# First stage of a ternary feed-forward kernel: indices and identities by the vector engine, maxima over partitions by the tensor engine, c of block 0 scaled by a bound, x loaded first

## The reference, cut to what matters

```python
def ternarize(W, threshold):
    absW = jnp.abs(W)
    delta = threshold * jnp.max(absW)
    mask = absW > delta
    n = jnp.maximum(jnp.sum(mask), 1)
    alpha = jnp.sum(jnp.where(mask, absW, 0.0)) / n
    return alpha * jnp.sign(W) * mask
c = jnp.einsum('bct,bcd->bdt', x, weights[conditions])   # weights gathered per batch
h = jnp.einsum('bsd,hd->bsh', c, ternarize(W1, 0.05)) + b1
h = jax.nn.gelu(h, approximate=False)
y = jnp.einsum('bsd,hd->bsh', h, ternarize(W2, 0.05)) + b2
scale = jnp.max(jnp.abs(y)) / 7 + 1e-8
out = x + jnp.clip(jnp.round(y / scale), -7, 7) * scale
```

## Time and profile before

| | us |
|---|---|
| three runs | 1043.31, 1045.27, 1045.33 (median 1045.27) |
| the profiled execution | 1043.61, its span 1041.8 |
| PE busy | 937.6 (90%) |
| DVE busy | 648.8 (62%) |
| ACT busy | 553.8 (53%) |
| POOL busy | 157.8 (15%) |

### The profile page before, as it was taken

The page is one execution under the profiler, slowest core; times in us unless marked ns, Lnnn a source line. Parts: engine busy times, 40 slices in busy tenths (PEclk is TensorE's granted clock), DMA queues, the critical chain, the costliest instruction groups (busy, mean ns, idle before and its releaser), DMA issues.

```text
span 1041.8 us, 15013 instructions
## 1 busy us (share of the span) xinstructions
PE 937.6 (90%) x5265; PEld 448.1 (43%) x5265; DVE 648.8 (62%) x1007; ACT 553.8 (53%) x710; POOL 157.8 (15%) x213
## 2 busy tenths in 40 slices
PE   0499999999999999999999999999999999999600
PEld 0355444444444444444444444444444444444200
DVE  3599766666666656666665666566666656633492
ACT  3489372727456473828274564638282645535290
POOL 4032303030110203030302102030303021000000
PEclk9899999999999999999999999999999999999855
DMA  6610120301121211203011112121030121105999
GB/s 219 201 44 4 30 63 11 70 21 40 45 45 41 50 40 43 48 10 78 13 40 45 45 40 50 40 50 41 10 81 10 40 47 44 40 0 181 307 386 376
DMA packets 40592, 77.89 MB, mean 75 GB/s; under 512 B 3952, under 2 KB 4352, under 8 KB 40064
## 3 DMA queue, kind: packets, MB, share of 16 engines
q1 hardware_dynamic: 36304, 73.47, 24.3%
q0 software_dynamic: 4096, 3.94, 1.4%
q10 hardware_dynamic: 176, 0.27, 0.1%
HBM read 60.89 MB, written 16.78 MB: 75 GB/s over the span
## 4 chain that ended last, share of the span: by engine, by line
PE 77%; issue 10%; ACT 5%; DVE 3%; POOL 2%; DMA 1%; DVEq 0%; ACTq 0%; SPq 0%; POOLq 0%
PE ps L444 38%; PE ps L456 35%; PE ps L432 3%; ACT y L692 2%; PE ps L474 1%; ACT y L664 1%; POOL ws L356 1%; DVE st L709 1%; DMA yx<-in_x 1%; DVE y L822 0%; DVE y L960 0%; ACT ps L692 0%; DVE wts L819 0%; DMA condb<-in_itok_B 0%; DVE st L768 0%
## 5 line engine op out<-in xcount | busy, mean ns | idle before, releaser
L444 PE MATMUL ps<-yc,wts 128*128 128x512 f16 x2048 | 447.3, 379 | 0.3 <-ACT g L596 0.3
L456 PE MATMUL ps<-wts 128*128 128x512 f16 x1920 | 419.3, 379 | 0.7 <-ACT wts L620 0.7
L444 PEld LDWEIGHTS ps<-yc,wts 128*128 128x128 f16 x2048 | 199.4, 98 | 238.7 <-ACT g L596 0.8
L456 PEld LDWEIGHTS ps<-wts 128*128 128x128 f16 x1920 | 185.8, 98 | 220.4 <-ACT wts L620 0.9
L742 DVE SCALAR_TENSOR_TENSOR wts<-g,st,wts 128x512 f16<-128x512 f32 x256 | 186.4, 749 | 143.0 <-ACT wts L601 141.1
L596 ACT ACTIVATE g<-ps,b1t,st 128x512 f32<-128x512 f32 x256 | 197.8, 773 | 116.7 <-PE ps L444 109.3
L601 ACT ACTIVATE wts<-g,st 128x512 f16<-128x512 f32 x256 | 181.0, 713 | 0.0
L583 ACT ACTIVATE xs<-yx,st 128x2048 f16<-128x2048 f32 x28 | 56.1, 2002 | 145.0 <-DVE st L777 145.0
L378 POOL PARTITION_ALL_REDUCE st<-st x46 | 21.5, 467 | 669.1 <-DVE st L711 413.6
L356 POOL DMA_INDIRECT wg<-in_L_cond_weights,ids x112 | 106.5, 951 | 41.3 <-issue 29.3
L747 DVE SCALAR_TENSOR_TENSOR y<-ps,st,b2b 128x512 f32 (+1 forms) x56 | 41.9, 748 | 78.0 <-PE ps L456 78.0
(11 more groups left out here) (118 smaller groups left out, 377.2 us busy)
## 6 DMA issues: line engine op xcount, KB each, us to landing
yx<-in_x SPq DMA_DIRECT2D x56, 512.0 KB, 6.1
out<-wts SPq DMA_DIRECT2D x12, 512.0 KB, 10.2
y<-in_x SPq DMA_DIRECT2D x5, 1024.0 KB, 10.0
wts<-in_x SPq DMA_DIRECT2D x10, 512.0 KB, 6.0
y<-in_L_ffn_W SPq DMA_DIRECT2D x8, 512.0 KB, 9.0
wts<-in_x SPq DMA_DIRECT2D x4, 1024.0 KB, 5.6
y<-in_L_ffn_W SPq DMA_DIRECT2D x4, 1024.0 KB, 8.0
out<-y SPq DMA_DIRECT2D x4, 1024.0 KB, 12.5
```

What stands on the lines that cost most here:

```text
L444: last = nc.tensor.matmul(psH[:, j % HB, :], T1T[:, k, j * P:(j + 1) * P], csp[:, a, k, :], start=(k == 0 and a == 0), stop=(k == KT - 1 a ...
L456: last = nc.tensor.matmul(psY[:, r % 2, :], hsp[:, a, j, r * P:(r + 1) * P], T2T[:, j, :], start=(j == 0 and a == 0), stop=(j == HT - 1 an ...
```

## The change

Everything lies ahead of the loop over blocks, or in the step of block 0.

- x of block 0 is loaded first, in four transfers of 256 KB (two on SP, two on ScalarE's queue after the list of conditions), then W1. W2 follows without a wait. b2's transfer goes behind ScalarE's absolutes.
- VectorE builds indices and identities, by scans, a 32 x 32 transpose and comparisons. GpSimd has no iota, no identity and no reduction of W1's maxima or of c of block 0 any more; it keeps the reduction of b1's.
- The gathers of blocks 0 and 1 are four instructions of 128 rows each instead of eight of 64. No diagonal is cleared. `condition_direct` multiplies 64 rows by 64 columns, sixteen matmuls a half, the two sides of the partitions in two banks.
- The maximum of a column over partitions: VectorE widens it to 128 columns (`wide`), TensorE transposes it (`all_partitions`), VectorE reduces it.
- c of block 0 isn't measured: its scale comes from 128 times the product of the powers of two of max|x| and max|w|. Both parts of it are made from PSUM directly.
- W1's masks come in eight chunks of two tiles (`masks1`). Three turns, not six, stand ahead of `first(0, 0)`, and the counts stand behind first 0, 1 and 2.
- W2's count is made by 32 matmuls (`count2`), ahead of second(0, 0), and ScalarE's sums go. `condition(1, 0)` moves from before the last four turns to behind second(0, 0), `condition(1, 1)` behind second(0, 1).

```diff
-    AHEAD = 6
-    TURNS2 = {10: (0, 1), 11: (2, 3), 12: (4, 5), 13: (6, 7), 14: (8, 9), 15: (10, 11)}
+    MASKED = 2
+    COUNTS1 = {0: (0,), 1: (1, 2), 2: (3,)}
+    AHEAD, EARLY = 3, 6
+    AFTER = {0: [(1, 3)], 1: [(1, 4)], 2: [(1, 5)], 3: [(1, 6), (1, 7)], **{j: [(1, j + 4)] for j in range(4, 12)}}
+    for j, more in {8: (0,), 9: (1,), 10: (2, 3), 11: (4,), 12: (5, 6), 13: (7, 8), 14: (9, 10), 15: (11,)}.items():
+        AFTER[j] = AFTER.get(j, []) + [(2, n) for n in more]
+    STORES = [1] * 8 + [2] * 6 + [1] * 2
...
@@ sync
-            sp.dma_start(condb[:, :], cond.rearrange("(a b) -> a b", a=1).to_broadcast([P, B])).then_inc(cond_loaded, 16)
+            load_direct(0, (0,))
             for c in range(LOADS):
                 sp.dma_start(w1s[:, c * HL:(c + 1) * HL, :], W1_v[:, c * HL:(c + 1) * HL, :]).then_inc(w1_loaded[c], 16)
-            load_direct(0)
-            sp.wait_ge(w_gathered[1], 16 * HALF)
             for n in range(RT):
                 sp.dma_start(w2s[:, n, :], W2_v[:, n, :]).then_inc(w2_loaded[n], 16)
+            sp.wait_ge(delta1_ready, 1)
             load_half(0, DIRECT * BB)
...
@@ gpsimd
+            pool.wait_ge(idx_made, 1)
+            gather_direct(0)
...
-            all_max(max1_part, 1, mx1r, mx1, max1_all)
-            all_max_c(0)
+            all_max(b1max_part, 1, mx1r[:, 1:2], mx1[:, 1:2], b1max_all)
+            gather_direct(1)
             pool.wait_ge(sum1_part, 1)
...
@@ tensor
+            def condition_direct(b, half, bank):
+                for k in range(KT):
+                    for j in range(2):
+                        for s in range(2):
+                            side = slice(s * C, (s + 1) * C)
+                            last = nc.tensor.matmul(bank[:, s, k, j * C:(j + 1) * C],
+                                                    xdirect[b][side, 2 * half + j, k * P:(k + 1) * P],
+                                                    wdirect[side, b, 2 * half + j, :], start=True, stop=True)
+                last.then_inc(c_made, 1)
+            def all_partitions(q, wide):
+                nc.tensor.transpose(psM[:, q, :], wide, idf).then_inc(wide_turned, 1)
+            def count2():
+                pe.wait_ge(t2_made, WCH)
+                for n in range(RT):
+                    for c in range(WCH):
+                        hc = slice(c * T, (c + 1) * T)
+                        nc.tensor.matmul(psN, ones[:, :], tern2[:, n, hc], start=(n == 0 and c == 0), stop=False)
+                        last = nc.tensor.matmul(psN, twos[:, :], neg2[:, n, hc], start=False,
+                                                stop=(n == RT - 1 and c == WCH - 1))
+                last.then_inc(n2_counted, 1)
...
             pe.wait_ge(b1_ready, 1)
-            pe.wait_ge(c_copied, 1)
-            count1(0)
-            count1(1)
-            for j in range(HC):
+            for j in range(AHEAD):
                 turn1(j)
-            count1(2)
-            count1(3)
-            for j in range(HC, AHEAD):
-                turn1(j)
-            pe.wait_ge(c_copied, 2)
+            pe.wait_ge(c0_split, 4)
             for j in range(HT):
...
-                if AHEAD + j < HT:
-                    turn1(AHEAD + j)
-                for n in TURNS2.get(j, ()):
-                    turn2(n)
-            condition(1, 0, direct=True)
+                for c in COUNTS1.get(j, ()):
+                    count1(c)
+                for weight, n in AFTER[j]:
+                    turn1(n) if weight == 1 else turn2(n)
             for j in range(TURNED, HT):
                 turn2(j)
+            pe.wait_ge(n_read, 1)
+            count2()
             pe.wait_ge(w_stored, 2 * HT)
...
@@ scalar
+            for c in range(5):
+                absolute(c)
+            high_c0(0, psCd)
+            absolute(5)
+            absolute(6)
+            high_c0(1, psCd0)
+            absolute(7)
+            act.dma_start(b2b[:, :], b2.rearrange("(a n) -> a n", a=1).to_broadcast([P, T])).then_inc(b2_loaded, 16)
...
@@ vector
+            dve.wait_ge(xdirect_loaded, 64)
+            link(nc.vector.tensor_reduce(mxw0[:, 0:1], xdirect[0], AX.XY, ALU.max, apply_absolute_value=True))
+            wide(wide_x, mxw0[:, 0:1])
+            max_w1(0)
...
+            max_w1(1)
+            dve.wait_ge(wd_gathered[0], 16 * RT)
+            link(nc.vector.tensor_reduce(mxw0[:, 1:2], wdirect[:, 0, :, :], AX.XY, ALU.max, apply_absolute_value=True))
+            wide(wide_w, mxw0[:, 1:2])
+            max_w1(2)
...
+            for c in range(3, LOADS):
+                last = max_w1(c)
+            link(last)
+            link(nc.vector.tensor_reduce(m1, wm1, AX.X, ALU.max))
+            wide(wide1, m1)
+            dve.wait_ge(cscale_ready, 1)
+            low_c0(0, 0, psCd)
...
             dve.wait_ge(w1abs_made, LOADS)
-            for c in range(3):
-                mask_w1(c)
-                positive_w1(c)
-            max_c(0, link)
-            mask_w1(3)
-            scale_c(0, link)
-            positive_w1(3)
-            low_c(0)
+            masks1(0)
+            low_c0(0, 1, psCd)
+            low_c0(1, 0, psCd0)
+            low_c0(1, 1, psCd0)
+            for c in range(1, HT // MASKED):
+                masks1(c)
```

More of the change, by code:

```diff
@@ L252, in _, with load_direct @@
         def _(sp):
-            def load_direct(b):
-                sp.dma_start(xdirect[b], x_v[:, b * RT:(b + 1) * RT, :]).then_inc(xdirect_loaded, 16)
+            def load_direct(b, sides):
+                for s in sides:
+                    for to, rows in direct(b, s):
+                        sp.dma_start(to, rows).then_inc(xdirect_loaded, 16)
             def load_half(n, first_batch):
@@ L411, in _, with condition @@
         def _(pe):
-            def condition(b, half, direct=False):
-                if direct:
-                    pe.wait_ge(xdirect_loaded, 16 * b + 16)
-                    pe.wait_ge(w_gathered[half], 16 * HALF * (b + 1))
-                else:
-                    pe.wait_ge(x_split, 2 * (b - DIRECT) + half + 1)
-                if not (direct and b == 0):
-                    pe.wait_ge(c_copied, 2 * b + half)
+            def condition(b, half):
+                pe.wait_ge(x_split, 2 * (b - DIRECT) + half + 1)
+                pe.wait_ge(c_copied, 2 * (b - 1) + half)
                 for k in range(KT):
                     tk = slice(k * P, (k + 1) * P)
-                    if direct:
-                        for j in range(RT // 2):
-                            r = half * RT // 2 + j
-                            o = (psC0 if b == 0 and half == 1 else psC)[:, k, j * P:(j + 1) * P]
-                            last = nc.tensor.matmul(o, xdirect[b][:, r, tk], wdirect[:, r, :], start=True, stop=True)
-                        continue
                     for j in range(HALF):
@@ new lines, in _ @@
+            link(nc.vector.transpose(turned32[:, 0:32], turned32[:, 32:64]))
+            nc.vector.tensor_copy(pcol, turned32[:, 0:1])
+            nc.vector.tensor_tensor_scan(ramp, ones_f, ones_f, -1.0, ALU.mult, ALU.add)
+            link(nc.vector.tensor_scalar(upper, turned32[:, 0:1], float(C), float(-C), ALU.is_ge, ALU.mult))
+            link(nc.vector.tensor_tensor(pc64, upper, pcol, ALU.add))
+            dve.wait_ge(cond_loaded, 16)
+            link(nc.vector.tensor_scalar(idt, condb[:, :], 0.0, float(S), ALU.is_lt, ALU.mult))
@@ new lines, in _ @@
+            link(nc.vector.tensor_tensor(idt, idt, condb[:, :], ALU.add))
+            link(nc.vector.tensor_scalar(idt, idt, 0.0, float(S - 1), ALU.max, ALU.min))
+            link(nc.vector.tensor_scalar(idx[:, :], idt, float(C), pc64, ALU.mult, ALU.add))
+            by_side = idx[:, 0:DIRECT * BB].rearrange("p (g s j) -> p s g j", s=2, j=2)
+            for s in range(2):
+                side = slice(s * C, (s + 1) * C)
+                last = nc.vector.tensor_copy(idsd[side, :, :].rearrange("p b (h j) -> p (b h) j", j=2), by_side[side, s, :, :])
```

285 lines of the change are left out of this document (164 added, 121 removed).

## The result

The changed kernel took 1052.45 us (median of 4 runs, 1051.20 to 1053.46) against 1044.64 (4 runs, 1043.31 to 1045.33) of the kernel before beside it: a ratio of 1.0075, 95% interval 1.0062 to 1.0087. It is slower by 7.8 us, where 2.4 faster was forecast; the time lies above the forecast's range. The profiled execution had 1053.46, its span 1051.3. Busy were TensorE 952.6 us, VectorE 655.5, ScalarE 544.5 and GpSimd 138.6.

A forecast was written before the change was run, and what follows sets the result against it. TensorE was taken as the bound after block 0's start; 90.3 + 29.4 + 1.85 put first(1, 0) at 121.6, 2.6 us earlier, rounded to 2.4, so 1044.4 - 2.4 = 1042.0 us, range 1038.8 to 1047.5.

The forecast's parts named there:

- What bounds the kernel: After block 0's start: TensorE is the bound, so any shift of first(1, 0), before at 124.20, reaches the end unchanged.
- Up to the threshold: Kernel start to W1's thresholds: VectorE is the chain, thresholds at 25.8 us against 38.7 before.
- rival (c): Start: x later than 8.3 or w later than 14.0 delays everything; 2 us gives 1044.1; chance 0.18, a third slower.
- near 20.7: Block 0's conditions: time in us when c is done, against 24.5 with weight loads in line mostly at low clock.
- To the first gelu: Threshold to first gelu: 20.5 us against 19.4 before, gelu at 46.3, so the gain shrinks from 12.9 to 11.9.
- Rival (a): Before first(0, 0): TensorE's clock stays high, saving 2.15 us more, 1039.9; chance 0.17.
- To `second(0, 0)`: First gelu to second(0, 0): 36.6 us as before plus 0.5, last turn 83.4, then count2 6.9, ending at 90.3.
- To `first(1, 0)`: From second(0, 0): 29.4 us as before plus 1.85 for another half condition, first(1, 0) at 121.6, 2.6 earlier.
- rival (b): Conditions: weight loads run in line, 3.7 us a half, 1046.7, or 1044.6 with high clock; chance 0.25, half slower.
- the estimate of 3.4 us: Half conditions: 64 rows load as slowly as 128, about 107 ns a load, 3.4 us a half.
- Chances: Whole kernel: forecast 0.40, (a) 0.17, (b) 0.25, (c) 0.18; faster 0.44, slower 0.20, no change 0.36.

The follow-up runs named there:

- e4_x_alone: Changed kernel with condition(1, 1) left late and only block 2's first x prepared early on GpSimd, VectorE and ScalarE: 1044.59 us, ratio 1.0001 to the kernel before.
- e10_alone: Changed kernel with SP's loads of W1 and W2 held back until block 0's four gathers have landed: 1055.94 us, one run.
- e5_turns_late: Changed kernel with W2's turns on TensorE put back in their places of before the change: 1050.27 us, ratio 1.0053 to the kernel before.
- e1_both_early: Changed kernel with both half conditions of block 1 directly behind second(0, 0): 1051.58 us, ratio 0.9993 to the kernel before.
- e2_gather_first: Changed kernel with block 2's gathers ahead of the reduction of c of block 1 on GpSimd: 1058.57 us, ratio 1.0067 to the kernel before.
- e8_sums_turns_c: Changed kernel with both block 1 half conditions behind second(0, 0), ScalarE's sums replacing count2, and W2's turns as before: 1036.86 us, ratio 0.9923 to the kernel before.
- e3_before_late: Kernel before with only condition(1, 1) moved from behind second(0, 0) to behind second(0, 1): 1057.17 us, ratio 1.0062 to the kernel before.
- e6_scalar_sums: Changed kernel without count2, ScalarE summing W2's absolutes as before the change: 1053.36 us, ratio 1.0027 to the kernel before.

## Why the prediction was wrong, point by point

**What bounds the kernel.** The step that failed is that "an offset of the first multiplication of block 1 [...] goes unchanged into the end", together with the line that settles the late c: "its copy, maximum and split take 9.7 after condition(1,1), which has two seconds, 13.8, to hide under". It put what the moved condition costs behind `first(1, 0)` at nothing; the runs showed 5.4 us of waiting and 2.0 at the low clock. The line on c is true, and e4_x_alone shows it. But it follows only the one consumer that the diff is about. Behind c's maximum, in the orders of GpSimd, VectorE and ScalarE, stands x of block 2, with its own end in block 1. The evidence stood in the rows: the 0.3 us of the earlier trace rows, which I took as a sign that nothing but TensorE matters there, was that relay arriving 0.34 us late. It means that this relay had no slack. Every microsecond by which x is delayed against `first(1, 0)` is waited in full, and the table above shows it to a hundredth.

**Up to the threshold.** Forecast 25.8, measured 27.35. Mis-sized were x (8.3 forecast, 9.7 measured; by e10_alone more than half of it its own transfer) and the gathers' landing (at most 3.8, measured 5.6 to 5.9, under W1's traffic: rival (c) in its milder form). They cost 1.9 us of VectorE's waiting for w. Too dear was the maximum of a part of W1: 1.34 each, measured 5.71 for five; the rows of before had timed its transfers, not VectorE. So two errors of opposite sign leave 1.55, in part by luck. No code load ahead of the gathers: right. Not in this sum are the two half conditions of block 0: 64 records took 7.09 us, 0.11 each, and c of block 0 was done at 25.02, where "near 20.7" was counted on. It cost nothing, narrowly: ScalarE's last absolute of W1, behind the high part of c, ended at 27.34, and the thresholds were there at 27.35.

**To the first gelu.** `first(0, 0)` 31.7 in 3.5 us, measured 33.09 in 3.42; last count 43.1, measured 44.3; gelu 46.3, measured 47.35. The lengths were right, and of the 1.4 us of delay at `first(0, 0)` 1.05 were left at the gelu. Rival (a), the clock that stays high, did not come.

**To `second(0, 0)`.** Forecast 83.4 for the last turn, measured 86.6. The wait for W2's first ternary part was foreseen at 4 us (3.72) and priced at 0.5, since TensorE would catch up. It did not: the unit behind the wait took 3.38 us at a granted clock of 0.58. With the turns moved (e5_turns_late) the last one was done at 83.1. Then `count2`, 6.9 forecast and 6.9 measured, all of it in the way: right.

**To `first(1, 0)`.** Each half condition costs 1.93 and 1.94 us (1.84 forecast, 3.7 by rival (b)). Its weight loads do last as long as before although they have half the rows:

```profile
L434 PEld LDWEIGHTS ps<-ws,y 64*128 64x128 f32 x64 | 3.7, 188 | 0.8 <-issue 0.8
```

188 ns against 192. But 32 of them passed in 1.93, one each 0.06. The Trainium skill says that a load's time does not go by its rows (TensorE: Matmul & The Clock Gate, LDWEIGHTS); the recorded lengths agree, 188 against 192. It also says that different tiles of the array load and multiply in parallel (TensorEngine Tiling (Array Packing), Key Properties); the pace of 0.06 agrees with it, and the estimate of 3.4 us from the first rule alone was wrong. That the two halves of the rows are what lets the loads overlap isn't shown: before, loads of all 128 rows with 192 ns each followed each other at 0.115, too, so the recorded length isn't the pace, and 64-row loads without a change of side weren't run. `first(1, 0)` came at 125.00 and not 121.6: 1.1 from the start, 2.1 from the turns, 0.2 from the conditions and small rests. Without the relay the kernel would so have been level with before, which e4_x_alone (1.0001) and e1_both_early (0.9993) show; the forecast would have been some 2.4 us off. The other 7.4 us are the relay, 5.4 and 2.0.

**Chances.** 0.20 stood for slower, all of it in the start and the weight loads. The rival that came was not among them. The forecast did name its own test: "no wait of TensorE that was not there". The ends of its range are not what its own terms give: (a) with both conditions at 1.0 would be 1038.2 and not 1038.8, (b) with a microsecond of (c) 1047.7 and not 1047.5; neither matters here.

## What to carry to other kernels

When an operation moves later, follow each engine's order behind its consumers, not only its consumers: what is queued behind them may feed the block after the next. A single short wait of the bounding engine was the most informative row here, because it marked a relay without slack; write down which transfer and which engines it runs over before moving anything ahead of it. A wait of the bounding engine costs more than its length when the clock falls in it: here a wait of 5.75 us brought 2.0 more.

## What the runs showed of the hardware

GpSimd's wait for the reduction's code came only together with an iota. With iota and reduction over partitions in a kernel, 9.6 and 9.2 us passed after the two markers; with an iota of 8 columns 8.7 and 6.0; with the reduction alone 0.1. Gathers ahead of the reduction don't bring it: four ran in the changed kernel. For a first call to loaded code the Trainium skill (GPSIMD Engine Reference, Instruction dispatch) has about 6 us: one of the four agrees and three were longer. With the reduction alone 0.1 passed; whether its code had to be loaded then, the trace doesn't tell.

The granted clock in the records does not always tell the pace. In the changed kernel it reads 1.00 from 28 to 37 us:

```profile
34.00:34.50 0.50, 0.50 (x3) 0.22 (x2) 0.50 (x2) 0.50 (x2) 0.00 (x0) 1.00 1.06 221
```

while `first(0, 0)`, from 33.09, had eight matmuls in 3.42 us, which take 1.89 from 37.66 on. By pace this is the low level. So it is in the conditions of block 0: 0.11 each from 17.93 on, 0.06 each from 100.30 on, and 1.00 is recorded in both places. Why the record differs stays open.

Also open are ScalarE's copy in e2_gather_first that came 3.1 us late, and the low clock in `second(0, 0)` of e8_sums_turns_c (it starts at 85.41 and lasts 8.89 us and not 7.07), which would be the next 1.8 us to gain, an estimate from these two lengths. e3_before_late and e6_scalar_sums have such a stretch at the same place, the kernel before and the changed one don't; what decides it wasn't tested.
